# Perceiver and Mamba block on one core: the loop over tiles written out, and six pieces of work moved in the order of a tile

## What is computed

```
x = x + xattn(v=ctx, k=ctx, q=layernorm(x), mask)         # 16 heads of 32, 257 keys
x = x + mamba(layernorm(x))                                # 1024 channels, 16 states
x = x + ffn(layernorm(x))                                  # 512 -> 2048 -> 512, quantised

mamba:  x_, z = split(x @ in_proj_w)
        x_ = silu(conv(x_, 4 taps, causal) + conv_b)
        Bm, C, dt = x_ @ x_proj_w;   dt = softplus(dt * dt_w + dt_b)
        h[t] = exp(dt * A) * h[t-1] + dt * x_ * Bm;   y = sum over states(h * C) + x_ * D
        out = (y * silu(z)) @ out_proj_w
```

## Time and profile before

| | |
|---|---|
| median of 3 runs | 2072.73 us (2072.69 to 2077.51) |
| profiled execution | 2073.24 us, span 2071.3 us |
| busy, share of the span | TensorE 92%, VectorE 87%, ScalarE 78%, GpSimd 27% |
| mean granted TensorE clock | 0.966 of full speed |
| instructions | 44099 |
| DMA | 200.18 MB, mean 97 GB/s |

### The profile page before, as it was taken

One profiled execution on the slowest core, in us unless ns is written; L12 is line 12 of the kernel. 1 busy time (PEld: TensorE's weight loads), 2 busy tenths in 40 slices (PEclk: granted clock), 3 DMA queues, 4 the chain that ended last, 5 costly groups with the idle time before them and its releaser, 6 DMA issues. The chain is left out here.

```text
span 2071.3 us, 44099 instructions
## 1 busy us (share of the span) xinstructions
PE 1899.4 (92%) x14989; PEld 1310.1 (63%) x15004; DVE 1793.2 (87%) x2207; ACT 1620.9 (78%) x4441; POOL 554.9 (27%) x435
## 2 busy tenths in 40 slices
PE   8898999999999899999899999989998999677799
PEld 5576666656676666666576766656665767366544
DVE  1546999989999898989899998989898999989788
ACT  3358888887978888888879797888888798867484
POOL 1001314141323233241413233331414142211013
PEclk9999999999999999999999999999999999788899
DMA  8623443333443433343344434343443433330214
GB/s 282 219 78 89 91 100 87 100 82 98 89 103 73 101 85 79 100 88 101 81 101 88 101 73 104 82 81 98 88 101 81 104 85 95 92 98 11 71 41 142
DMA packets 97677, 200.18 MB, mean 97 GB/s; under 512 B 17380, under 2 KB 40308, under 8 KB 92280
## 3 DMA queue, kind: packets, MB, share of 16 engines
q1 hardware_dynamic: 76376, 133.32, 20.5%
q0 software_dynamic: 21024, 63.45, 17.0%
HBM read 116.12 MB, written 17.18 MB: 64 GB/s over the span
## 5 line engine op out<-in xcount | busy, mean ns | idle before, releaser
L1487 ACT ACTIVATE dA<-dt,A_sb 128x124 f32<-128x124 f32 x2048 | 618.8, 401 | 5.1 <-DVE dt L1819 5.0
L1875 DVE TENSOR_TENSOR_SCAN hb<-dA,hb 128x2048 f32<-128x2048 f32 x118 | 522.2, 4425 | 11.9 <-ACT dA L1487 8.5
L1021 PE MATMUL bank<-wv_sb,ctxT 128*128 128x512 f32 x1024 | 470.6, 600 | 2.3 <-ACT ctxT L1297 2.3
L1010 PE MATMUL bank<-ctxT,wk_sb 128*128 128x256 f32 x2048 | 462.5, 383 | 3.7 <-ACT ctxT L1297 3.6
L1010 PEld LDWEIGHTS bank<-ctxT,wk_sb 128*128 128x128 f32 x2048 | 382.8, 191 | 64.2 <-ACT ctxT L1297 10.4
L1597 POOL DMA_DIRECT2D hb<-hb x117 | 105.2, 899 | 853.9 <-DVE hb L1881 827.1
L1021 PEld LDWEIGHTS bank<-wv_sb,ctxT 128*128 128x128 f32 x1024 | 186.5, 191 | 191.0 <-issue 185.6
L1870 DVE TENSOR_TENSOR hb<-u,BC 128x2048 f32<-128x2048 f32 x118 | 270.0, 2288 | 6.6 <-DVE u L1832 2.6
L1881 DVE TENSOR_TENSOR hb<-hb,BC 128x2048 f32<-128x2048 f32 x117 | 268.2, 2293 | 1.5
L1119 PE MATMUL bank<-xn2T,win_sb 128*128 128x128 f32 x2048 | 250.2, 286 | 3.2 <-ACT xn2T L1393 3.2
L1119 PEld LDWEIGHTS bank<-xn2T,win_sb 128*128 128x128 f32 x2048 | 247.3, 202 | 8.6 <-ACT KT L1313 3.6
(11 more groups left out here) (171 smaller groups left out, 2490.1 us busy)
## 6 DMA issues: line engine op xcount, KB each, us to landing
hb<-hb POOLq DMA_DIRECT2D x103, 512.0 KB, 5.1
ctx_sb<-in_ctx_dram SPq DMA_DIRECT2D x64, 512.0 KB, 3.8
BC<-bcd_dram SPq DMA_DIRECT2D x32, 1024.0 KB, 6.9
maskb<-in_mask_Bx1x1xS_fk_dram SPq DMA_DIRECT2D x64, 128.5 KB, 3.3
wstage<-in_L_ffn_w_dram SPq DMA_DIRECT2D x4, 2048.0 KB, 11.7
x_sb<-in_x_dram SPq DMA_DIRECT2D x16, 256.0 KB, 3.4
win_sb<-in_L_attn_in_proj_w_dram SPq DMA_DIRECT2D x1, 4096.0 KB
bo_sb<-bias_dram SPq DMA_DIRECT2D x64, 64.0 KB, 2.2
```

The costliest lines, as they stand in the source:

```text
L1010: last = pe.matmul(bank[6 + j][:, (m % 2) * KF:(m % 2 + 1) * KF], wk_sb[:, c, m * P:(m + 1) * P], ctxT[:, c, :], start=(c == 0), stop=(c = ...
L1021: last = pe.matmul(bank[h][:], ctxT[:, c, h * P:(h + 1) * P], wv_sb[:, c, :], start=(c == 0), stop=(c == DC - 1))
L1487: last = act.activation(dA[:, c % 2, n * BT:(n + 1) * BT, 1:], dt[:, c, :].rearrange("p (b s) -> p b s", s=S)[:, :, 1:], ACT.Exp, scale=A_ ...
L1875: ins = dve.tensor_tensor_scan(flat, dA[:, c % 2].rearrange("p n s -> p (n s)"), flat, 0.0, ALU.mult, ALU.add)
```

## The change

The hardware loop over intervals 3 to 14 becomes a loop of the program that writes the kernel, so every engine's stream holds these twelve intervals one after the other. Inside an interval:

- step 25 of the chain, (6, 2), moves from place "b" to place "c" of slot 0, which lies behind `mamba_conv`
- `keys_copy(g + 1, 1)` moves behind `mamba_turn` and `mamba_transpose` in slot 0
- `mamba_skip` moves from ahead of `values_copy(g + 1, 0)` to behind `weigh_values` in slot 3
- `q_transpose` moves ahead of `values_copy(g + 1, 1)` in slot 2
- `mamba_keep` moves ahead of places "d" and "e" in slot 3
- `out_sum` and `out_norm` move behind place "e" in slot 1, which holds step 3 of the chain, (1, 0)

```diff
--- before.py
+++ after.py
@@ -332,7 +332,7 @@
         CHAIN.append((IC - 1, 3))
         DONE = {step: k + 1 for k, step in enumerate(CHAIN)}
         DONE[IC - 1, 3] += 1
-        FINISH = {(0, "x"): range(20, 21), (0, "a"): range(21, 22), (0, "b"): range(22, 26), (0, "c"): range(26, 28),
+        FINISH = {(0, "x"): range(20, 21), (0, "a"): range(21, 22), (0, "b"): range(22, 25), (0, "c"): range(25, 28),
                   (1, "a"): range(28, 29), (1, "t"): range(29, 31), (1, "p"): range(31, 32)}
         BEGIN = {(1, "b"): range(0, 1), (1, "d"): range(1, 3), (1, "e"): range(3, 4), (2, "a"): range(4, 5),
                  (2, "b"): range(5, 7), (2, "c"): range(7, 9), (2, "d"): range(9, 11), (2, "e"): range(11, 12),
@@ -548,11 +548,11 @@
                         part.normalise(g)
                     if b > 0:
                         place("n")
-                    if following:
-                        part.keys_copy(g + 1, 1)
                     if b == 0 and front:
                         part.mamba_turn(tm, keys)
                         part.mamba_transpose(tm, keys)
+                    if following:
+                        part.keys_copy(g + 1, 1)
                     if b == 0:
                         place("n")
                     place("k")
@@ -585,8 +585,6 @@
                     place("p")
                     if b == 3 and back:
                         part.out_rows(to)
-                    if b == 3 and front:
-                        part.mamba_skip(tm)
                     if b == 1 and front:
                         part.rows_load(tm, 1)
                     if following and b > 0:
@@ -604,6 +602,8 @@
                         part.mamba_u(tm, (1,))
                     if here:
                         part.weigh_values(g, ta, b, tm)
+                    if b == 3 and front:
+                        part.mamba_skip(tm)
                     if b == 0 and here and not front:
                         part.last_values()
                     if b == 0 and front:
@@ -617,25 +617,26 @@
                         part.gate_silu(tm)
                     if following:
                         part.kv_values(g + 1, 1, range(DC))
+                    if b == 2 and here and more:
+                        part.q_transpose(ta + 1)
+                    if following:
                         part.values_copy(g + 1, 1)
                     if b == 0 and front:
                         part.mamba_table(tm)
-                    if b == 2 and here and more:
-                        part.q_transpose(ta + 1)
+                    if b == 3 and front:
+                        part.mamba_keep(tm)
                     place("d")
+                    place("e")
                     if b == 1 and back:
                         part.out_sum(to)
                         part.out_norm(to)
-                    place("e")
-                    if b == 3 and front:
-                        part.mamba_keep(tm)
                     if b == 3 and back:
                         part.out_transpose(to, keys)
 
             interval(0, None, None, True)
             interval(1, 0, None, True)
             interval(2, 1, 0, True)
-            with engine.Fori(3, NT - 1) as t:
+            for t in range(3, NT - 1):
                 interval(t, t - 1, t - 2, True)
             interval(NT - 1, NT - 2, NT - 3, False)
             tail(part)
```

## The result

The changed kernel takes a median of 1997.85 us in 4 runs (1995.94 to 1998.8); the kernel before, on the same chip, 2072.71 us (2072.56 to 2077.51). The ratio is 0.9632 (95% interval 0.9616 to 0.9649): 74.9 us less, against 66.7 forecast, and inside the range of 1993 to 2026 us, toward its fast end. The profiled execution took 1995.94 us with a span of 1994.2, 77.1 us shorter than the span before. In the parts of the engines every line of the changed file is one higher than before: L1780 is the old L1779.

What follows compares the result with a forecast made beforehand. Each pass was bound by VectorE, then ScalarE and TensorE, then VectorE, plus the loop's turn. Twelve intervals at 108.1 us gain 64.9, intervals 2 and 15 another 2.3; 67.2 off 2073.2 gives 2006 us, range 1993 to 2026.

Steps and rivals of the forecast that it cites:

- The loop's turns: Between passes of intervals 3 to 14: writing the loop out removes 11 turns and VectorE's stalls there, 41.5 us.
- the straight interval: One interval in straight code, from one x1 sum to the next, taken as 110.06 us; twelve make 1320.72.
- The rival by which the stalls aren't the loop's: VectorE's stalls at the handovers stay, and the edits save only 0.7 us an interval: 2063 us, chance 0.04.
- (d): Slower rival: straight code stalls on VectorE where instructions are fetched; at six stalls an interval 2114 us, chance 0.04.
- Convolution, xn2's copy and the second residual sum: Slots 0 to 2: earlier SiLU and scores of slot 2, VectorE's waits for TensorE filled: 2.1 us an interval.
- The copy of x1: End of an interval: GpSimd's earlier copy removes VectorE's 0.51 us wait but may hold it up: 0.2 us gained.
- Skip products and V's copies on ScalarE: Slot 3 and handover: oT comes earlier and TensorE's 1.10 us wait goes, but VectorE is the bound: worth nothing.
- The clock: Behind handovers: TensorE's clock dips at one of three, a third of 1.33 us, booked as 0.35 us lost an interval.
- The rival (a): The clock dips at every handover because TensorE waits for ScalarE there: 13.7 us more, 2020 us, chance 0.17.
- the 107.31: Best interval in us: no clock dip, with the full 2.24 and 0.51 us gained; the kernel at about 1993 us.
- The signs that I had named: Trace marks on VectorE, ScalarE and TensorE: vanished or shorter waits and intervals near 108 us if right, others if wrong.
- (b): Rival: only the turns pay, the moved work meets a new wait, such as mid-convolution: 2032 us, chance 0.13.

Runs made afterwards that it cites:

- experiment 1: The kernel before with only its loop over intervals 3 to 14 written out, nothing moved: 2023.74 us, ratio 0.9769.
- Experiment 3: The kernel before with two intervals in each pass of the hardware loop, 6 passes and 5 turns: 2051.55 us, ratio 0.99.
- experiment 9: The kernel before with the loop written out and only step (6, 2) moved behind the convolution: 2005.23 us, ratio 0.967.
- experiment 5: The changed kernel with step (6, 2) put back ahead of the convolution: 2025.84 us, ratio 0.9782.
- experiment 7: The changed kernel with the skip products (mamba_skip) put back ahead of the first copy of V in slot 3: 1992.81 us, ratio 0.9612.
- experiment 10: The changed kernel with ScalarE's three moves (keys_copy, mamba_skip, q_transpose) undone: 2002.29 us, ratio 0.9659.
- experiment 6: The changed kernel with out_sum and out_norm put back ahead of place "e": 1996.53 us, ratio 0.9632.
- experiment 4: The changed kernel with mamba_keep, the copy of x1, put back behind places "d" and "e": 1996.54 us, ratio 0.9632.
- experiment 12: The changed kernel with the skip products put back and GpSimd's copy of x1 issued twice in a row: 1996.23 us, ratio 0.9636.
- experiment 8: The changed kernel with nine unread matmuls of 128 columns on TensorE ahead of the context's turn in slot 0: 1993.65 us, ratio 0.9618.

## Why the prediction was right, and where its terms were off

**The loop's turns** (booked 41.5). Right in kind, and it was three fifths of the result: 44.3 us in the profile of experiment 1. The term was under-sized by 2.8 us through its base, the straight interval, booked at 110.06 and measured at 109.83. I had taken the first pass of the loop for straight code, and it was slower by small steps up to the scores of slot 2 (experiment 1). Experiment 3 shows the price going with the number of turns. The rival by which the stalls aren't the loop's is out: a turn cost about 4 us of the kernel's time. By the Trainium skill's "Advanced Engine Details and Errata", section "Control Flow Timing", the eleven turns would have been worth 1.8 us, an estimate from its figures for two kinds of branch; the traces don't agree. Another page of the Trainium skill, "Runtime: NRT & Kernel Launch", section "Instruction fetch mechanics", says that a taken branch to a place that isn't in the instruction memory forces a fetch before execution can go on. The traces agree in what they show: the profile's lines on the DMA queues that carry instructions, of the kernel before (queue, packets, MB, share),

```profile
q8 instruction: 140, 2.29, 0.4%
q14 instruction: 137, 1.12, 0.2%
```

and of the changed one:

```profile
q8 instruction: 117, 1.92, 0.4%
q14 instruction: 74, 0.61, 0.1%
```

The kernel before brings in 3.41 MB of instructions, the changed one, with its twelve intervals in a row, 2.53. With five turns (experiment 3) it is 2.98, so each turn goes with another 0.08 to 0.09 MB. That the stall is this fetch and not something else of the turn was not tried by itself. The slower side (d), stalls in straight code, didn't come: VectorE has no "issue" wait longer than about 0.2 us.

**Convolution, xn2's copy and the second residual sum** (booked 2.1 together, bounds 0 and 2.24). Together they give 2.34, a little beyond the upper bound, but they share it otherwise than I had it. The convolution alone gives 1.62 (experiment 9). xn2's copy ahead of K's, which "makes room for the 2.2 us above and counts nothing by itself", gives 0.72 once the convolution is early and nothing before that, as I had it (experiments 5, 7 and 10): TensorE no longer waits for SiLU, runs without a wait from L1120 to the scores of slot 2, and L1120 starts 0.68 us sooner. What I had not seen is ScalarE's part: in experiment 10 its taps come 0.72 us later, and the convolution, which I had down as never late, waits 0.20 us for them in its middle and then goes at their pace. The residual sum, to which I gave the 1.65 us of L1965's wait, gives nothing (experiment 6): the same early TensorE had removed that wait already (experiment 9). I had seen both stalls as one chain through TensorE, and still booked a second cure for it. The upper bound was the sum of these two waits. It was no bound: VectorE's waits for the folding DMA are slack in the same stretch, and what the moves can give is how much sooner TensorE comes to the scores, 64.27 - 61.93 = 2.34 us. That 2.1 was near is partly luck.

**The copy of x1** (booked 0.2, bounds -0.09 and 0.51). Measured 0.47 without a dip. Its size was off because the wait it removes is 0.67 us in straight code (I had taken the 0.51 of one handover); start to start that is 0.75, and 0.31 of it is given back at L1985. That the middle of my bounds came to 0.3 for this (0.51 less 0.2) was luck. Experiments 4 and 12 show a hold-up of 0.31 and 0.41 us a copy, in one or two small instructions, less than the 0.60 us of the shortest copy and much less than the 1.6 us that the copy lasts in its new place. The Trainium skill ("SBUF — State Buffer", section "SBUF: two separate sides") has the shared port pair as an exclusive lock for a whole instruction. The traces agree in that the copy and the instruction held up end together: the copy at 325.05 + 1.62 = 326.67, L1985 at 326.69. The full 0.60, with which I had got a loss of 0.09 us, wasn't the price.

**Skip products and V's copies on ScalarE** (booked at nothing). The step that failed. I asked what oT's earlier arrival would bring VectorE (nothing, right), and not what TensorE would do with the time. It starts L1082 1.2 us sooner, but the context's turn behind it still waits for the second copy of V, which comes when it came before (0.17 and 0.15 us ahead of x1's sum, experiment 7). So TensorE stands still there for 1.44 us in one piece, where it had waited 1.02 us ahead of L1082 and 0.17 at the turn. In the interval that gap costs nothing by itself: 107.03 us with it and without. By the clock it costs 1.0 us each time the clock falls, and it fell at eight of thirteen handovers of the changed kernel, at none when the skip products were put back (experiment 7) or the gap filled (experiment 8). The medians put 4 to 5 us on it (1997.85 against 1993.65 and 1992.81, with intervals of the ratios that still overlap), where eight dips at 1.0 would be 8; in the profile of experiment 7 VectorE waits longer for the folding DMA, which takes part of it back.

**The clock** (booked 0.35 an interval). The dips came, but from this new gap and not left over from the earlier trace rows: experiment 1 has none at its thirteen handovers from 335.00 us on, only the one inside interval 2 that the earlier trace rows show, and the changed kernel hasn't that one. (My reading of it was loose too: the low clock begins at 243.9 us, just ahead of the 0.51 us gap that I named.) That a third of 1.33 us came near an average of the right order was luck. The twelve intervals together lie 1293.03 - 12 x 107.03 = 8.7 us above the best, 0.72 each, of which seven dips make up 7 and the longer waits for the folding DMA most of the rest. The rival (a), a dip at every handover, was half true, and cheaper than the 1.33 us that I took. A dip costs its 1.0 us by way of TensorE, which comes to slot 2's scores that much later: they start 395.44 - 332.53 = 62.91 us behind x1's sum, beside 61.93 without a dip. Why the clock fell at only some of the handovers with the same gap, and in experiment 5 at none of thirteen, stays open.

**Start and tail** (booked at nothing). The first x1 sum shown comes 6.2 us earlier, the tail takes 1.7 us more. Over fourteen profiles that start lies between 224.9 and 231.65 us. The three kernels with a hardware loop have it at 229.3, 230.3 and 231.65, ten of the eleven written out at 224.9 to 228.3, and the eleventh, experiment 8, which has its extra matmuls there too, at 231.1. The medians also ask for some 4 us outside the pipeline: 74.9 less its 72.7, plus the tail's 1.7, is 3.9. So about 4 us at the start seem to go with the loop, well before its first pass; no run shows why, and my sum did not have them. The rest of the 6.2 is a matter of the two executions that were profiled.

In sum, the sixteen-tile pipeline gave 69.2 + 3.5 = 72.7 us where I had booked 67.2, and the terms of an interval, with what was measured, are 109.83 - 2.34 - 0.47 + 0.72 = 107.74 against the 108.1 booked. The base, the moves and the copy were each booked too small a gain, by 0.23, 0.24 and 0.27, and the clock too small a loss, by 0.37. An interval without a dip, 107.03 us, is shorter than the 107.31 that I had called the best.

**The signs that I had named.** No "issue" waits: so. L1147 without a wait, L1780 right behind the product: so. SiLU's wait under 0.4 and slot 2's under 0.3: missed by little, 0.59 and 0.41. A granted clock below 1.00 at most handovers, the sign against me: at eight of thirteen, but at 1.0 us each. A gap in the middle of the convolution, the sign of (b): there, 0.46 us, in the intervals with a dip and in no other, too small to carry (b).

## What to carry over

Where a wait is booked to nothing that the profile shows, at the same place in each pass of a hardware loop, compare it with the same code outside the loop first: here it was 44 of 77 us, and moves of work inside the loop were worth next to nothing until it was gone. When an engine gets its work sooner, look at what it waits for next: if that doesn't come sooner too, small waits gather into one, and a gap that cost nothing in the chain of waits cost 1.0 us each time the clock fell behind it. Of several edits that cure one chain, book one, and for the next only what the first leaves.

## What the hardware showed that I had not expected

- A gap of 1.44 us on TensorE was followed by the lower clock and one of 1.46 at the next handover was not. With nine unread matmuls, 2.27 us of work more an interval, the kernel took 4.2 us less (1993.65 against 1997.85; the intervals of the ratios overlap: 0.9605 to 0.9631 and 0.9616 to 0.9649).
- GpSimd's copy of 128x512 made a VectorE instruction of 0.13 us last 0.50, and the two next to it no longer than elsewhere.
- The moves inside the loop's body were worth 0.2 us an interval, and 2.8 in straight code.
